# A scan on TensorE with split fp32r operands: two of its ten passes per output half joined in one pass on stacked rows

## The chip, the cores and the metric

The kernel runs on one core of a Trainium2 chip. TensorE (PE in the profile, with PEld for its weight loads) multiplies, VectorE (DVE), ScalarE (ACT) and GpSimd (POOL) do the elementwise work, and SyncE (SP) issues most DMAs. The engines run their own instruction streams and wait for each other through semaphores. The metric is the device time of one launch in microseconds. The kernel before took 4611.31 us, the median of three runs (4606.82 to 4611.5).

## The reference, cut to what matters

Two blocks follow each other. The first is the one that the change touches: it normalizes each 7 by 7 window of the image over its 192 channels, runs a linear recurrence over the 49 tokens of the window, and puts an MLP behind it.

```python
x = x + _L0_conv_ref(_gn(x), A, Bm, Cm, ...)     # block 1, group norm before it
x = x + _L1_conv_ref(_gn(x), qkv_w, ...)         # block 2, window attention

# inside block 1, w holds 1024 windows x 49 tokens x 192 channels:
w = _ln(w, ln1_w, ln1_b)
xs = jnp.swapaxes(w @ Bm, 0, 1)
h = xb + h @ A            # the scan, 49 steps, one after the other
w = h @ Cm
y = _ln(xr, ln2_w, ln2_b)
y = gelu(y @ W1 + b1) @ W2 + b2
return xr + y
```

## The kernel before

**Precision by parts.** An fp32 operand is held as an upper part rounded to fp32r and a lower part, what is left. A product is made from upper by upper, upper by lower and lower by upper. The contraction runs over 192 channels, which are 128 ("a") and 64 ("b"). `Split` keeps four weight tiles of 128 rows, `a_hi`, `a_lo`, `b_hi`, `b_lo`, and `Split.terms` lists five passes: (a_hi, da), (a_hi, dl), (a_lo, da), (b_hi, db), (b_lo, db). In the data tile slot 0 is the upper part of the first 128 channels; slot 1 holds the upper part of the last 64 channels in rows 0 to 63 and their lower part in rows 64 to 127. `b_hi` has the weights of those 64 channels twice, so that one pass takes both.

**Slots.** The scan has 49 steps, and each is cut in two chunks of 512 windows, so block 1 has 98 slots; the inner ones are a hardware loop (`Fori`), two slots a turn. Every engine has its own `slot(t, c)`, a list written out by hand with the pieces of several slots interleaved. Nothing but these lists and the semaphores sets the order. With n the slot's number, TensorE does in slot n:

1. the scan's sum for chunk step n+1 into `ps_h` (L618: two output halves of 128 and 64 channels, each 5 passes of `W_B` on xn and 5 of `W_A` on the state h, 20 in all, 512 columns each),
2. the transposes of `yb` into `ps_g` (L589, L591),
3. the second half of the MLP's second layer of n-1 into `ps_o` (L603),
4. the MLP's first layer, 30 passes into `ps_g` (L634), which wait for the lower parts of y (`s_yl`),
5. the state times `W_C` into `ps_r` (L645),
6. the transposes of `xn` of n+2 into `ps_h`,
7. the first half of the second layer (L603), which waits for all lower parts of the gelu's output (`s_gld`, `s_glp`).

The other engines, as far as the argument goes:

- ACT takes `ps_h` to `h_hi` with a bias (L401, `s_hh`), then `ps_g` to `y_hi` (L390, L391), then six gelus and their upper parts (L415, L420), then `ps_h` to `xn_hi` (L390, L391, `s_xh`).
- DVE normalizes the next tokens (L500 multiplies `xt` by a table, L502 subtracts another), makes the lower parts of h (L481) and of y (L479), finishes the output `x1` of the slot before (L488, L491, `s_x1`), then statistics and gelu lower parts (L531, L536, L543), then statistics of `ps_r` (L549, L554, L557), the lower parts of xn (L479), `res` (L564), `yb` (L568), and the other half of `x1` (L488, L491).
- POOL forms `res` (L442) and two reciprocal roots (L447, L456; the latter waits for L557), two gelu lower parts (L452), and behind L456 the square of `x1` and two running sums (L463, L465, L468).
- SP sends `x1` out in 14 DMAs as soon as `s_x1` says so (L379) and then loads the next `xt` (L351), in that order.

Of the kernel before, what the change touches and what calls it, by code (L numbers as in the profile page):

```python
# [7 lines left out]
fp32 = mybir.dt.float32  # L8
f32r = mybir.dt.float32r
# [47 lines left out]
def build(nc, x, A, Bm, Cm, ln1, ln2, W1, b1, W2, b2,  # L57
# [6 lines left out]
    with top:  # L64
# [31 lines left out]
        with ExitStack() as ctx:  # L96
# [6 lines left out]
            R1 = sb("R1", [P, NT, C])  # L103
            M1 = sb("M1", [P, NT, C])
            W_B, W_A, W_C = (Split(ctx, name, C) for name in ("wB", "wA", "wC"))
            W_1 = Split(ctx, "w1", HID)
            w2 = sb("w2", [P, FT, 2, C], f32r)
            b2b = sb("b2b", [P, C])
# [6 lines left out]
            with ExitStack() as pre:  # L115
# [49 lines left out]
                @block.gpsimd  # L165
                def _(pool):
                    pool.memset(acc_x[:, :, :], 0.0)
                    pool.memset(acc_x2[:, :, :], 0.0)
                    pool.memset(neg_half[:, :], -0.5).then_inc(s_i0, 1)
                    pool.wait_ge(s_i0, 1)  # L170

                    pool.wait_ge(s_wh, 1)
                    for full, parts in ((fold_B, W_B), (raw_A, W_A), (raw_C, W_C), (fold_1, W_1)):
                        for t in range(2):
                            pool.tensor_tensor(parts.parts[2 * t + 1][:, :], full[:, t, :],
                                               parts.parts[2 * t][:, :], ALU.subtract)
                    pool.tensor_tensor(w2[:, :, 1, :], raw_2[:, :, :], w2[:, :, 0, :], ALU.subtract)

                    pool.wait_ge(s_fold, 11)
                    pool.tensor_tensor(gtab[:, 0, :, :], gvar[:, :, :],  # L180
                                       neg_half[:, :].rearrange("p (a b) -> p a b", a=2), ALU.pow).then_inc(s_pow, 1)

                @block.vector
                def _(dve):
                    fold = [0]

                    def link(ins):

                        fold[0] += 1
                        ins.then_inc(s_fold, 1)  # L190
                        dve.wait_ge(s_fold, fold[0])

                    for k in range(NT):
                        if k == NT // 2:

                            dve.wait_ge(s_w, 16 * WEIGHT_LOADS)
                            for t in range(2):
                                dve.tensor_scalar(fold_B[:, t, :], raw_B[:, t, :], l1[:, t, 0:1], None, ALU.mult)
                                last = dve.tensor_scalar(fold_1[:, t, :], raw_1[:, t, :], l2[:, t, 0:1], None,
                                                         ALU.mult)  # L200
                            link(last)
                        dve.wait_ge(s_xs[k % XS], 16 * (k // XS + 1))
                        for g in range(GROUPS):
                            last = dve.bn_stats(st[:, GROUPS * k + g, :], xs[k % XS][:, :, CG * g:CG * (g + 1)])
                        last.then_inc(s_bn, 1)
                    dve.wait_ge(s_bn, NT)
                    per = T * CG / 2
                    link(dve.tensor_tensor(pm[:, 0, :], st[:, :, 1], st[:, :, 4], ALU.add))
                    link(dve.tensor_tensor(sq[:, 0, :], st[:, :, 1], st[:, :, 1], ALU.mult))
                    link(dve.tensor_tensor(sq[:, 1, :], st[:, :, 4], st[:, :, 4], ALU.mult))  # L210
                    link(dve.tensor_tensor(sq[:, 0, :], sq[:, 0, :], sq[:, 1, :], ALU.add))
                    link(dve.tensor_tensor(sq[:, 1, :], st[:, :, 2], st[:, :, 5], ALU.add))
                    link(dve.scalar_tensor_tensor(out=pm[:, 1, :], in0=sq[:, 1, :], scalar=1.0 / per,
                                                  in1=sq[:, 0, :], op0=ALU.mult, op1=ALU.add))

                    dve.wait_ge(s_sum, 1)
                    dve.tensor_copy(hbias[:, 0:1], ps_g[:, 0:1])
                    dve.tensor_copy(hbias[0:CB, 1:2], ps_g[0:CB, 1:2])
                    link(dve.tensor_tensor(b1f[:, :], ps_g[:, 8:8 + FT], b1c[:, :], ALU.add))
                    dve.wait_ge(s_sum, 2)  # L220
                    sums = ps_h[:, 0:8].rearrange("p (a h q) -> p a h q", a=2, h=2)
                    link(dve.tensor_scalar(gmean[:, :, :], sums[:, 0], 0.5, None, ALU.mult))
                    link(dve.tensor_tensor(gtab[:, 1, :, :], gmean[:, :, :], gmean[:, :, :], ALU.mult))
                    dve.scalar_tensor_tensor(out=gvar[:, :, :], in0=sums[:, 1], scalar=0.5,
                                             in1=gtab[:, 1, :, :], op0=ALU.mult, op1=ALU.subtract).then_inc(s_tab, 1)
                    dve.wait_ge(s_tab, 1)
                    link(dve.tensor_scalar(gvar[:, :, :], gvar[:, :, :], GN_EPS, None, ALU.add))
                    dve.wait_ge(s_pow, 1)
                    link(dve.tensor_tensor(gtab[:, 1, :, :], gmean[:, :, :], gtab[:, 0, :, :], ALU.mult))
                    link(dve.tensor_copy(gwide[:, :, :], gtab[:, :, :, :].rearrange("p a h q -> p (a h q)")  # L230
                                         .unsqueeze(2).to_broadcast([P, 8, WINS])))

                    dve.wait_ge(s_sum, 3)
                    for a, tab in enumerate((R1, M1)):
                        last = dve.tensor_copy(tab[:, :, :].rearrange("p k (g e) -> p (k g) e", e=CG),
                                               ps_g[:, 256 * a:256 * (a + 1)].unsqueeze(2)
                                               .to_broadcast([P, NT * GROUPS, CG]))
                    link(last)
# [40 lines left out]
            h_hi = [sb(f"h_hi{b}", [P, 2, NTOK], f32r) for b in range(2)]  # L279
            h_lo = [sb(f"h_lo{b}", [P, NTOK], f32r) for b in range(2)]  # L280
            yb = sb("yb", [P, TPC, C])
            y_hi, y_lo = sb("y_hi", [P, 2, NTOK], f32r), sb("y_lo", [P, NTOK], f32r)
            gF = [sb(f"gF{b}", [P, NTOK]) for b in range(4)]
            g_hi, g_lo = (sb(name, [P, FT, NTOK], f32r) for name in ("g_hi", "g_lo"))
# [27 lines left out]
            s_st1, s_ag1, s_ve1 = sem("ln1_stats"), sem("ln1_aggregated"), sem("ln1_var_eps")  # L312
            s_rs1, s_xn = sem("ln1_rstd"), sem("xn_ready")
            s_t1, s_xh, s_xl = sem("xn_transposed"), sem("xn_hi_ready"), sem("xn_lo_ready")
            s_scan, s_hh, s_hl = sem("scan_summed"), sem("h_hi_ready"), sem("h_lo_ready")
            s_cm, s_res, s_rsum = sem("mixed"), sem("residual_ready"), sem("residual_summed")
            s_st2, s_ag2, s_ve2 = sem("ln2_stats"), sem("ln2_aggregated"), sem("ln2_var_eps")
# [68 lines left out]
            def _(act):  # L386
# [6 lines left out]
                def slot(t, c):  # L393
# [13 lines left out]
                    if there(n):  # L407
                        for f in range(FT):
                            act.wait_ge(s_w1, FT * n + f + 1)
                            if f == 0:  # L410
                                upto(act, s_w2, n)
                            elif f >= 4:

                                act.wait_ge(s_gld, len(LO_DVE) * n + LO_DVE.index(f - 4) + 1)
                            act.activation(gF[f % 4][:, :], ps_g[:, f % 2, :], ACT.Gelu,  # L415
                                           bias=b1f[:, f:f + 1]).then_inc(s_gelu, 1)

                            for g in range(max(f - 1, 0), f + (f == FT - 1)):
                                act.wait_ge(s_gelu, FT * n + g + 1)
                                act.activation(g_hi[:, g, :], gF[g % 4][:, :], ACT.Copy).then_inc(s_gh, 1)  # L420
                    if there(n + 2):
                        act.wait_ge(s_t1, n + 3)
                        upto(act, s_scan, n + 1)
                        upper_parts(xn_hi[c], ps_h).then_inc(s_xh, 1)

                slots(act, slot)

            @block.gpsimd
            def _(pool):
                for c in range(2):  # L430
                    pool.memset(h_hi[c][:, :, :].bitcast(fp32), 0.0)
                    last = pool.memset(h_lo[c][:, :].bitcast(fp32), 0.0)
                last.then_inc(s_init, 1)

# [148 lines left out]
            def _(pe):  # L583
# [23 lines left out]
                def slot(t, c):  # L607
                    n = CHUNKS * t + c
                    if there(n + 1):

                        d = 1 - c
                        pe.wait_ge(s_xl, n + 2)
                        upto(pe, s_hl, n)
                        for m, rows in enumerate((P, CB)):
                            cols = slice(P * m, P * m + rows)
                            terms = (*W_B.terms(xn_hi[d], xn_lo[d], cols), *W_A.terms(h_hi[d], h_lo[d], cols))
                            for k, (w, v) in enumerate(terms):
                                last = pe.matmul(ps_h[0:rows, m, :], w, v, start=(k == 0), stop=(k == len(terms) - 1))  # L618
                        last.then_inc(s_scan, 1)
# [769 lines left out]
```

## Time and profile before

| what | us |
| --- | --- |
| median of three runs | 4611.31 |
| profiled execution, whole | 4597.89 |
| profiled execution, span from first to last instruction | 4596.1 |
| block 1, from the first xn (L500) to the last x1, about | 155 to 2430 |

The page of the profile gives busy time per engine over the span: PE 94%, weight loads 80%, DVE 86%, ACT 54%, POOL 56%. These are means over two very different blocks; only block 1 is touched by the change, so the rows of block 1 are the ones to read. A row of a timeline gives the start, the duration, the engine, the line and the shapes; what stands in brackets is how long the engine sat idle ahead of it and who ended that. A row of the windows gives the stretch and its length, then busy us and number of instructions of PE, PEld, DVE, ACT and POOL, then the granted TensorE clock as a share of full speed, the DMA share and GB/s. A busy matmul engine is shown by overlapping rows: a pass of 512 columns lasts 0.39 us in the trace, but the next one starts before it ends.

### The profile page before, as it was taken

The page shows a single profiled execution, that of the slowest core. Times are in us where ns is not written, and L with a number is a line of the kernel's source. Part 1 is how long each engine was busy: PE and PEld are TensorE (multiplying, and loading weights), DVE is VectorE, ACT ScalarE, POOL GpSimd, SP SyncE. Part 2 cuts the span into 40 slices and gives each one's busy share as a digit, 9 for nine tenths or more (in the row PEclk, how much of TensorE's full clock was granted, in tenths as well). Part 3 has the DMA queues.
Part 4 walks back from the last instruction along what each step waited for, and adds up shares of the span by engine and source line. Part 5 has one row for each costly group of instructions (what it writes and reads, how often), then busy time and mean ns, then how long its engine had stood idle before and what let it go on. Part 6 is the DMA issues. An engine that isn't in the chain of part 4 may idle for free. (4 is left out here: it accounts for less than half of the span.)

```text
span 4596.1 us, 142253 instructions
## 1 busy us (share of the span) xinstructions
PE 4316.2 (94%) x52232; PEld 3688.3 (80%) x52232; DVE 3933.2 (86%) x8105; ACT 2476.2 (54%) x4852; POOL 2584.1 (56%) x2092
## 2 busy tenths in 40 slices
PE   0599999999999999999995999999999999999998
PEld 0488888888888888888885888888888888888887
DVE  6698888888888888888872888888888888888888
ACT  0244444444444444444441666777776766776676
POOL 1155555555555555555542666666666666666666
PEclk9999999999999999999996999999999999999999
DMA  8011111111111111111111222222222222222222
GB/s 354 17 39 39 39 39 39 39 39 39 40 41 39 39 39 39 39 39 39 39 34 46 71 76 74 75 74 74 74 76 75 75 75 75 74 74 74 74 74 69
DMA packets 389849, 286.06 MB, mean 62 GB/s; under 512 B 147147, under 2 KB 388091, under 8 KB 388603
## 3 DMA queue, kind: packets, MB, share of 16 engines
q1 hardware_dynamic: 387060, 283.20, 21.2%
q10 hardware_dynamic: 2736, 2.14, 0.1%
q8 instruction: 35, 0.57, 0.1%
q14 instruction: 18, 0.15, 0.0%
HBM read 120.39 MB, written 87.31 MB: 45 GB/s over the span
## 5 line engine op out<-in xcount | busy, mean ns | idle before, releaser
L892 POOL TENSOR_TENSOR L<-L,mx 128x588 f32<-128x588 f32 x512 | 600.3, 1172 | 644.0 <-DVE mx L1118 643.9
L603 PE MATMUL ps_o<-w,g_hi 128*128 128x384 f32 x2352 | 711.1, 365 | 5.9 <-DVE g_lo L543 4.1
L415 ACT ACTIVATE gF<-ps_g,b1f 128x512 f32<-128x512 f32 x588 | 404.7, 688 | 392.9 <-PE ps_g L634 390.8
L886 POOL TENSOR_TENSOR E<-E,ri 128x588 f32<-128x588 f32 x512 | 600.0, 1172 | 0.8 <-DVE ri L1124 0.8
L1180 PE MATMUL ps_s<-Kp,Q 32*64 32x98 f32 x12288 | 494.5, 259 | 59.9 <-DMA Kp<-K 58.8
L603 PE MATMUL ps_o<-w,g_lo 128*128 128x192 f32 x2352 | 535.0, 255 | 0.0
L442 POOL TENSOR_TENSOR res<-xt,b2b 128x768 f32<-128x768 f32 x98 | 181.1, 1848 | 591.2 <-DVE x L491 591.2
L401 ACT ACTIVATE h_hi<-ps_h,hbias 128x512 fp32r<-128x512 f32 x196 | 123.1, 679 | 703.7 <-PE ps_h L618 703.7
L1114 DVE SCALAR_TENSOR_TENSOR L<-ps_s,bias 128x588 f32<-128x588 f32 x512 | 394.6, 771 | 92.2 <-PE ps_s L1180 76.5
L603 PEld LDWEIGHTS ps_o<-w,g_hi 128*128 128x128 f32 x2352 | 429.9, 189 | 26.8 <-issue 24.8
L999 ACT ACTIVATE o_hi<-ps_v,vb 128x98 fp32r<-128x98 f32 (+1 forms) x1024 | 289.1, 334 | 300.5 <-PE ps_v L1293 293.3
L603 PEld LDWEIGHTS ps_o<-w,g_lo 128*128 128x128 f32 x2352 | 444.2, 191 | 0.0
L974 ACT ACTIVATE PT<-ps_t 98x588 f32<-98x588 f32 x512 | 342.6, 669 | 157.5 <-PE ps_t L1256 154.5
L1180 PEld LDWEIGHTS ps_s<-Kp,Q 32*64 32x64 f32 x12288 | 299.7, 130 | 145.8 <-issue 37.1
L1118 DVE TENSOR_REDUCE mx<-L 128x12 f32<-128x588 f32 x512 | 392.2, 766 | 17.5
L1293 PEld LDWEIGHTS ps_v<-PT,Vx 98*32 98x32 f32 x12288 | 310.9, 151 | 95.8 <-issue 66.4
L1122 DVE TENSOR_REDUCE sm<-E 128x12 f32<-128x588 f32 x512 | 386.4, 755 | 0.1
L1293 PE MATMUL ps_v<-PT,Vx 98*32 98x49 f32 x12288 | 374.8, 235 | 4.0 <-DVE o_hi L1099 2.8
L452 POOL TENSOR_TENSOR g_lo<-gF,g_hi 128x512 fp32r<-128x512 f32 x196 | 250.4, 1298 | 197.2 <-ACT g_hi L420 197.2
L420 ACT ACTIVATE g_hi<-gF 128x512 fp32r<-128x512 f32 x588 | 355.4, 621 | 0.0
L980 ACT ACTIVATE E<-L 128x588 f32<-128x588 f32 x512 | 351.4, 686 | 3.9 <-POOL L L892 0.8
L536 DVE TENSOR_SCALAR xn<-xn,mva,rsa 128x192 f32<-128x192 f32 x392 | 316.6, 869 | 2.3 <-POOL rsa L447 2.3
(222 smaller groups left out, 12495.5 us busy)
## 6 DMA issues: line engine op xcount, KB each, us to landing
xs<-in_x SPq DMA_DIRECT2D x8, 4704.0 KB, 22.2
xt<-in_x SPq DMA_DIRECT2D x98, 384.0 KB, 3.4
x_cells<-x SPq DMA_DIRECT2D x784, 48.0 KB
xb<-x_cells SPq DMA_DIRECT2D x128, 294.0 KB
Vx<-V SPq DMA_DIRECT2D x512, 73.5 KB
out<-yo SPq DMA_DIRECT2D x128, 294.0 KB
Kp<-K SPq DMA_DIRECT2D x256, 98.0 KB, 2.0
Kp<-K SPq DMA_DIRECT2D x256, 49.0 KB, 1.9
```

The lines of the kernel that those rows point to most:

```text
L415: act.activation(gF[f % 4][:, :], ps_g[:, f % 2, :], ACT.Gelu, bias=b1f[:, f:f + 1]).then_inc(s_gelu, 1)
L420: act.activation(g_hi[:, g, :], gF[g % 4][:, :], ACT.Copy).then_inc(s_gh, 1)
L603: last = pe.matmul(dst, g[:, f, P * k:P * (k + 1)], w, start=(f == 0 and i == 0), stop=(f == FT - 1 and i == 1))
L886: pool.tensor_tensor(e, e, ri[p][:, :].unsqueeze(2).to_broadcast([P, HEADS, T]), ALU.mult)\
L892: pool.tensor_tensor(l, l, mx[p][:, :].unsqueeze(2).to_broadcast([P, HEADS, T]), ALU.subtract).then_inc(s_sub, 1)
L974: act.activation(PT[lp % 2][0:T2, :, :].rearrange("p j (w t) -> p w j t", w=2), ps_t[0:T2, :, 0:JP * SLOT].rearrange("p w (j t) -> p w j t ...
L980: act.activation(E[pp][:, :, :], L[pp][:, :, :], ACT.Exp).then_inc(s_ex, 1)
L1114: dve.scalar_tensor_tensor(out=L[p][:, :, :].rearrange("p (a h) m -> p a (h m)", a=2), in0=ps_s[:, :, 0:SB], scalar=HD ** -0.5, in1=tab, o ...
L1118: dve.tensor_reduce(mx[p][:, :], L[p][:, :, :], AX.X, ALU.max).then_inc(s_mx, 1)
L1122: dve.tensor_reduce(sm[pp][:, :], E[pp][:, :, :], AX.X, ALU.add).then_inc(s_sm, 1)
L1180: last = pe.matmul(s_pair(j)[SLOT * w:SLOT * (w + 1)], Q[c][rows, chunk, 2 * p + w, :], Kp[c][rows, chunk, :, 2 * p + w, :], start=True, s ...
L1293: last = pe.matmul(ps_v[row:row + 2 * HD, col:col + T], Vx[lc][0:T2, 2 * lp + w, g:2 * HD * JP:JP], PT[lp % 2][0:T2, j, T * w:T * (w + 1)] ...
```

## The change

The lower weight parts of the last 64 input channels (`W_B.b_lo`) and of the last 64 state channels (`W_A.b_lo`) each use only 64 rows of data. The change stacks them: a new weight tile `W_AB_b_lo` has `W_B`'s 64 rows on top and `W_A`'s below, and a new data tile `xh_b` (two buffers) has the upper part of xn's last 64 channels on top and that of h's below. One pass on the two tiles takes the place of two, for both output halves, so a slot has 18 scan passes for 20.

For this ACT makes two more copies per slot (64 partitions by 512 columns): the part of h behind the last gelu upper part, ahead of `xn_hi`; the part of xn behind `xn_hi`. TensorE's scan waits for two more semaphores. Before block 1, DVE makes `W_AB_b_lo` with two subtractions where POOL made two `b_lo` tiles, and POOL clears two more buffers at the start of block 1.

```diff
             W_B, W_A, W_C = (Split(ctx, name, C) for name in ("wB", "wA", "wC"))
+            W_AB_b_lo = sb("wAB_b_lo", [P, C], f32r)
...
-                        for t in range(2):
+                        for t in range(1 if parts in (W_A, W_B) else 2):
                             pool.tensor_tensor(parts.parts[2 * t + 1][:, :], full[:, t, :],
                                                parts.parts[2 * t][:, :], ALU.subtract)
...
+                    dve.wait_ge(s_wh, 1)
+                    for full, parts, rows in ((fold_B, W_B, slice(0, CB)), (raw_A, W_A, slice(CB, P))):
+                        dve.tensor_tensor(W_AB_b_lo[rows, :], full[rows, 1, :], parts.parts[2][rows, :], ALU.subtract)
                     dve.wait_ge(s_sum, 1)
...
+            xh_b = [sb(f"xh_b{b}", [P, NTOK], f32r) for b in range(2)]
...
+                    if there(n + 1):
+                        act.wait_ge(s_hh, n + 2)
+                        act.activation(xh_b[1 - c][CB:P, :], h_hi[1 - c][0:CB, 1, :], ACT.Copy).then_inc(s_hs, 1)
                     if there(n + 2):
                         act.wait_ge(s_t1, n + 3)
                         upto(act, s_scan, n + 1)
                         upper_parts(xn_hi[c], ps_h).then_inc(s_xh, 1)
+                        act.wait_ge(s_xh, n + 3)
+                        act.activation(xh_b[c][0:CB, :], xn_hi[c][0:CB, 1, :], ACT.Copy).then_inc(s_xs, 1)
...
                 for c in range(2):
                     pool.memset(h_hi[c][:, :, :].bitcast(fp32), 0.0)
+                    pool.memset(xh_b[c][:, :].bitcast(fp32), 0.0)
...
                         pe.wait_ge(s_xl, n + 2)
+                        pe.wait_ge(s_xs, n + 2)
                         upto(pe, s_hl, n)
+                        upto(pe, s_hs, n)
                         for m, rows in enumerate((P, CB)):
                             cols = slice(P * m, P * m + rows)
-                            terms = (*W_B.terms(xn_hi[d], xn_lo[d], cols), *W_A.terms(h_hi[d], h_lo[d], cols))
+                            terms = (*W_B.terms(xn_hi[d], xn_lo[d], cols)[0:4], *W_A.terms(h_hi[d], h_lo[d], cols)[0:4],
+                                     (W_AB_b_lo[:, cols], xh_b[d][:, :]))
```

On TensorE the first output half of one scan in the steady part stood like this before (a row is a pass, `out<-data,weights`; numbers behind a tile's name are its buffer):

```order
L618 MATMUL ps_h<-xn_hi0,wB_a_hi 128x512 [waits h_lo_ready,xn_lo_ready]
L618 MATMUL ps_h<-xn_lo0,wB_a_hi 128x512
L618 MATMUL ps_h<-xn_hi0,wB_a_lo 128x512
L618 MATMUL ps_h<-xn_hi0,wB_b_hi 128x512
L618 MATMUL ps_h<-xn_hi0,wB_b_lo 128x512
L618 MATMUL ps_h<-h_hi0,wA_a_hi 128x512
L618 MATMUL ps_h<-h_lo0,wA_a_hi 128x512
L618 MATMUL ps_h<-h_hi0,wA_a_lo 128x512
L618 MATMUL ps_h<-h_hi0,wA_b_hi 128x512
L618 MATMUL ps_h<-h_hi0,wA_b_lo 128x512
```

The same place in the changed kernel, where the line is L633:

```order
L633 MATMUL ps_h<-xn_hi0,wB_a_hi 128x512 [waits h_lo_ready,h_b_hi_stacked,xn_b_hi_stacked,xn_lo_ready]
L633 MATMUL ps_h<-xn_lo0,wB_a_hi 128x512
L633 MATMUL ps_h<-xn_hi0,wB_a_lo 128x512
L633 MATMUL ps_h<-xn_hi0,wB_b_hi 128x512
L633 MATMUL ps_h<-h_hi0,wA_a_hi 128x512
L633 MATMUL ps_h<-h_lo0,wA_a_hi 128x512
L633 MATMUL ps_h<-h_hi0,wA_a_lo 128x512
L633 MATMUL ps_h<-h_hi0,wA_b_hi 128x512
L633 MATMUL ps_h<-xh_b0,wAB_b_lo 128x512
```

Ten passes have become nine; the second output half (64x512) changes in the same way. The first pass waits for two semaphores more, and nothing else on TensorE has moved.

On ACT the end of one slot stood like this before, from the last gelu upper part to the state's upper part of the next slot:

```order
L420 ACTIVATE g_hi<-gF1 128x512 [waits hidden_ready]
L390 ACTIVATE xn_hi0<-ps_h 128x512 [waits scan_summed,xn_transposed]
L391 ACTIVATE xn_hi0<-ps_h 64x512
L401 ACTIVATE h_hi0<-ps_h,hbias 128x512 [waits mixed,scan_summed]
L401 ACTIVATE h_hi0<-ps_h,hbias 64x512
L390 ACTIVATE y_hi<-ps_g 128x512 [waits y_transposed]
```

In the changed kernel:

```order
L426 ACTIVATE g_hi<-gF1 128x512 [waits hidden_ready]
L429 ACTIVATE xh_b1<-h_hi1 64x512 [waits h_hi_ready]
L396 ACTIVATE xn_hi0<-ps_h 128x512 [waits scan_summed,xn_transposed]
L397 ACTIVATE xn_hi0<-ps_h 64x512
L435 ACTIVATE xh_b0<-xn_hi0 64x512 [waits xn_hi_ready]
L407 ACTIVATE h_hi0<-ps_h,hbias 128x512 [waits mixed,scan_summed]
L407 ACTIVATE h_hi0<-ps_h,hbias 64x512
L396 ACTIVATE y_hi<-ps_g 128x512 [waits y_transposed]
```

One copy now stands ahead of `xn_hi`, in the place where ACT waits for TensorE's transposes, and one between `xn_hi` and the next state.

## Rows read from the trace of the kernel before

**Rows 1.** Busy time by engine (windows) in a stretch of block 1's steady part.

```profile
1000.00:1500.00 500.00, 499.97 (x2942) 430.90 (x2941) 443.77 (x940) 226.82 (x396) 251.65 (x177) 1.00 0.14 39
```

**Rows 2.** Timeline of PE and PEld, one scan and its neighbours, then the next first layer.

```profile
1215.86 0.39 PE L618 MATMUL ps_h<-xn_hi,wB_a_hi 128*128 128x512 f32 x1
...
1220.45 0.60 PE L589 MATMUL ps_g<-ident,yb 128*128 128x128 f32 x4
...
1224.92 0.19 PEld L634 LDWEIGHTS ps_g<-y_hi,w_a_hi 128*128 128x128 f32 x1 [0.24 <-DVE y_hi L479]
```

**Rows 3.** Timeline of ACT in the same slot.

```profile
1210.00 1.14 ACT L420 ACTIVATE g_hi<-gF 128x512 fp32r<-128x512 f32 x2
1212.42 0.60 ACT L390 ACTIVATE xn_hi<-ps_h 128x512 fp32r<-128x512 f32 x1 [1.28 <-PE ps_h L591]
1212.92 0.58 ACT L391 ACTIVATE xn_hi<-ps_h 64x512 fp32r<-64x512 f32 x1
1220.65 1.26 ACT L401 ACTIVATE h_hi<-ps_h,hbias 128x512 fp32r<-128x512 f32 x2 [7.15 <-PE ps_h L618]
```

**Rows 4.** Timeline of DVE in the same slot.

```profile
1210.92 1.28 DVE L543 TENSOR_TENSOR g_lo<-gF,g_hi 128x512 fp32r<-128x512 f32 x2
...
1213.87 0.68 DVE L479 TENSOR_TENSOR xn_lo<-ps_h,xn_hi 128x512 fp32r<-128x512 f32 x1
...
1219.57 1.38 DVE L500 TENSOR_TENSOR xn<-xt,R 128x768 f32<-128x768 f32 x1 [0.73 <-DMA xt<-in_x]
1220.98 0.96 DVE L502 TENSOR_TENSOR xn<-xn,M 128x768 f32<-128x768 f32 x1
1221.94 0.75 DVE L481 SCALAR_TENSOR_TENSOR h_lo<-ps_h,hbias,h_hi 128x512 fp32r<-128x512 f32 x1
...
1224.18 0.68 DVE L479 TENSOR_TENSOR y_hi<-ps_g,y_hi 64x512 fp32r<-64x512 f32 x1
...
1242.46 1.27 DVE L500 TENSOR_TENSOR xn<-xt,R 128x768 f32<-128x768 f32 x1 [0.83 <-DMA xt<-in_x]
```

**Rows 5.** Timeline of POOL, the last sum of this slot and of the next.

```profile
1218.27 1.87 POOL L468 TENSOR_TENSOR acc_x<-acc_x,x1sq 128x768 f32<-128x768 f32 x1
...
1241.06 1.86 POOL L468 TENSOR_TENSOR acc_x<-acc_x,x1sq 128x768 f32<-128x768 f32 x1
```

**Rows 6.** Timeline of DVE and ACT, the slot in which xt came latest.

```profile
308.21 0.96 DVE L500 TENSOR_TENSOR xn<-xt,R 128x768 f32<-128x768 f32 x1 [1.40 <-DMA xt<-in_x]
...
308.62 1.26 ACT L401 ACTIVATE h_hi<-ps_h,hbias 128x512 fp32r<-128x512 f32 x2 [7.15 <-PE ps_h L618]
...
309.20 0.96 DVE L502 TENSOR_TENSOR xn<-xn,M 128x768 f32<-128x768 f32 x1
...
310.08 0.74 DVE L481 SCALAR_TENSOR_TENSOR h_lo<-ps_h,hbias,h_hi 128x512 fp32r<-128x512 f32 x1
```

**Rows 7.** One tile (xn) from 1000 to 1500 us: duration ns min/median/max.

```profile
L500 DVE TENSOR_TENSOR xn<-xt,R x22: 1048/1270/1432, 1014.5 to 1493.1; 128x768 f32<-128x768 f32 x22
```

**Rows 8.** Groups by line, 1000 to 1500 us (busy, mean ns, idle before in all).

```profile
L481 DVE SCALAR_TENSOR_TENSOR h_lo<-ps_h,hbias,h_hi 128x512 fp32r<-128x512 f32 x22 | 16.5, 751 | 0.2
```

**Rows 9.** Timeline of DVE, the ramp's third scan, then block 1's last.

```profile
218.92 0.75 DVE L481 SCALAR_TENSOR_TENSOR h_lo<-ps_h,hbias,h_hi 128x512 fp32r<-128x512 f32 x1 [1.18 <-ACT h_hi L401]
...
2384.37 0.75 DVE L481 SCALAR_TENSOR_TENSOR h_lo<-ps_h,hbias,h_hi 128x512 fp32r<-128x512 f32 x1 [3.10 <-ACT h_hi L401]
```

**Rows 10.** Timeline of PE in the ramp's first scan.

```profile
167.18 0.80 PE L618 MATMUL ps_h<-xn_hi,wB_a_hi 128*128 128x512 f32 x1 [2.65 <-DVE xn_hi L479]
...
170.34 0.63 PE L618 MATMUL ps_h<-h_hi,wA_a_lo 128*128 128x512 f32 x1
170.76 0.60 PE L618 MATMUL ps_h<-h_hi,wA_b_hi 128*128 128x512 f32 x1
```

**Rows 11.** Timeline of DVE ahead of block 1.

```profile
142.76 0.16 DVE L222 TENSOR_SCALAR gmean<-ps_h 128x4 f32<-128x4 f32 x1 [1.71 <-PE ps_h L258]
```

**Rows 12.** Busy time by engine (windows) at block 1's end.

```profile
2395.00:2405.00 10.00, 8.56 (x63) 7.93 (x62) 7.48 (x20) 2.38 (x5) 7.02 (x5) 1.00 0.08 22
```

More of the change, by code:

```diff
@@ L314, in build @@
             s_t1, s_xh, s_xl = sem("xn_transposed"), sem("xn_hi_ready"), sem("xn_lo_ready")
+            s_xs, s_hs = sem("xn_b_hi_stacked"), sem("h_b_hi_stacked")
             s_scan, s_hh, s_hl = sem("scan_summed"), sem("h_hi_ready"), sem("h_lo_ready")
```

## The prediction

> **What bounds the kernel now.** I read the stretch windows first. From 1000 to 1500 us, a steady piece of block 1, TensorE is busy for 499.97 of 500 us, DVE for 443.77, ACT for 226.82 and POOL for 251.65 [rows 1]. Read alone, that says that TensorE is the bound and that every pass taken from it is time gained. Matmul records overlap, however, so this number cannot show small waits. So I went to the timelines and followed one slot, looking at each wait for what ends last.
>
> TensorE does wait. The first weight load of the MLP's first layer sits idle for 0.24 us until DVE's lower part of y is there (L479 ends at 1224.18 + 0.68 = 1224.86) [rows 2, 4]. DVE reaches that point by a fixed run of four pieces that starts with the lower part of h (L481) at 1221.94 [rows 4]. What lets L481 start? Two paths lead from the end of DVE's last gelu lower part (L543: 1210.92 + 1.28 = 1212.20) [rows 4] to this one instruction:
>
> - *Path T, by TensorE.* Half a second layer, then the scan from 1215.86, whose successor starts at 1220.45 [rows 2]; ACT makes the upper part of h from 1220.65 to 1221.91 [rows 3]; L481 starts 0.03 us behind it [rows 4].
> - *Path P, by POOL.* DVE's statistics, then POOL's root, square and two sums, the last of which ends at 1218.27 + 1.87 = 1220.14 [rows 5]. DVE's L500 ends at 1219.57 + 1.38 = 1220.95, then L502 at 1220.98 + 0.96 = 1221.94, and L481 starts at 1221.94 [rows 4].
>
> L500 is marked as having waited for its load, but its end is not set by that. It ends 0.81 us behind POOL's last sum here; one slot later, starting 0.10 us later against the slot, it ends at 1242.46 + 1.27 = 1243.73, again 0.81 us behind POOL's 1241.06 + 1.86 = 1242.92 [rows 4, 5]. Where the load comes so late that POOL is through, L500 takes 0.96 us [rows 6]; in the steady part it takes 1.05 to 1.43 [rows 7]. The excess of 0.09 to 0.47 us is time in which it cannot proceed beside POOL, and that much slack has the load. The Trainium skill, page "SBUF — State Buffer", section "Who interferes with whom", calls the port pair that the two engines share an exclusive lock; by that rule L500 would stand until POOL's sum is done, and the trace agrees.
>
> Behind L481 both paths are one again: y's lower parts, TensorE's first layer, gelus, POOL's gelu lower parts, L543. One turn takes 22.79 us (POOL's last sum starts at 1218.27 and at 1241.06) [rows 5]. Only path T contains the scan. So what the change is worth hangs on how much shorter path P is.
>
> **How much shorter path P is.** L481 starts 0.00 us behind the end of L502, on average 0.2 / 22 = 0.01 [rows 4, 8]. Where DVE has nothing to wait for, it starts earlier than that: in the slot with the late load ACT was through at 308.62 + 1.26 = 309.88, and L481 started at 310.08 while L502 ended at 309.20 + 0.96 = 310.16, that is 0.08 us ahead of the end [rows 6]. So in the steady slots L481 waits for ACT for about 0.08 us, and path P is shorter by that. It is a small difference read from one place, so its bounds are 0 (L481 is released by L502 already) and 0.10. I take 0.08.
>
> **The change part by part.**
>
> *Passes.* A pass costs (1220.45 - 1215.86) / 20 = 0.2295 us [rows 2]; four fewer take 0.92 us out of path T in each slot. Of this 0.08 us moves L481 forward; then path P ends last, and the other 0.84 us becomes a longer wait of TensorE ahead of the first layer: 0.24 + 0.84 = 1.08 us. There are 98 scans; three belong to the ramp and one is the last, so the steady term is 94 x 0.08 = 7.5 us, with bounds 0 and 9.4.
>
> *Ramp.* In the first three scans DVE waits for the state, in the third, where it waits least, for 1.18 us, which is more than 0.92 [rows 9]; no POOL sum is under way then. The passes there run at two rates. In the first scan the early ones come every 0.42 us (170.34 to 170.76), behind a wait of 2.65 us [rows 10]: the lower of the clock's two levels, against 0.2295. I take the rise of the clock as not moved by the change, so that fast passes fall away: 3 x 0.92 = 2.8 us. If slow ones fell away in two scans, it would be 2 x 1.7 + 0.92 = 4.3.
>
> *Last scan.* No further L500 stands in its way, and DVE waits 3.10 us for it [rows 9]: 0.9 us.
>
> *Copies on ACT.* The trace has no copy from SBUF to SBUF of this shape. The nearest rows are 0.58 us for 64 partitions from PSUM and 1.14 for two of 128 from SBUF [rows 3]. The first copy stands ahead of `xn_hi`, where ACT is idle for 1.28 us until TensorE's transposes end [rows 3]; it ends 0.7 us before them. Even when late it would cost nothing at first, as DVE takes up `xn_hi` at 1213.87, 0.37 us behind its end at 1213.50 [rows 3, 4]. Without any cover, 0.6 us would go into path T, which after the cut has 0.84 to give. The second copy ends near 1213.50 + 0.65 = 1214.15, and TensorE wants it at 1215.86 [rows 2, 3]; behind it ACT idles for 7.15 us in the row of before [rows 3]. Both cost 0. If a copy took 1.7 us instead, it would begin to hold DVE up; no row of ACT with 512 columns is near that.
>
> *Two more waits on TensorE's scan.* Both semaphores have risen 1.7 us earlier by the sum above. Bounds 0 and the few hundredths that a released instruction starts late, and these fall into the 1.08 us. Queued behind the scan's first pass are all of TensorE's passes; they have the same cover. Cost 0.
>
> *Ahead of block 1.* Two subtractions of 64x192 on DVE stand before a wait of 1.71 us for TensorE [rows 11]. Their nearest row is the one of 64x512, 0.68 us [rows 4]; two of that would be 1.36, so the wait hides them. POOL has less to do there and clears two more buffers while DVE waits for its first load. Cost 0.
>
> **Sum.** 7.5 + 2.8 + 0.9 = 11.2 us, with bounds 0 + 2.8 + 0.9 = 3.7 and 9.4 + 4.3 + 0.9 = 14.6. Against the profiled execution, 4597.89 us, that is 4586.7, or 0.24% less. The median of the runs shown is 4611.31, 0.3% above that execution; the same 11.2 us from it give 4600.
>
> **A rule weighed against the row.** By the matmul row, 499.97 of 500, TensorE is the bound and the sum would be 90 us (first rival). The Trainium skill, page "Perfetto Trace Analysis", section "Identifying the Most-Contended Engine", says that matmul occupancy is a bad measure and that the share of weight loads is a good one for TensorE, while occupancy is fair for the others. Here that is 430.90 / 500 = 86% against DVE's 443.77 / 500 = 89% [rows 1]: by that rule DVE is the most contended and a cut on TensorE alone gives about nothing. The chain read above lands nearer to the rule than to the row.
>
> **The rivals.**
>
> *TensorE is the bound after all.* Then each slot gains the whole 0.92 us: 94 x 0.92 + 3.7 = 90 us, 4521. For it: its wait of 0.24 us is 1% of a slot [rows 2]. Against it: L500 ends at the same distance behind POOL in both slots shown, and L502 ends where L481 starts; the POOL path would have to give way by itself. 6 in 100.
>
> *The two paths are equally long.* L481 is released by L502 as well, and only the ramp and the last scan gain: 3.7 us, 4607.6. For it: 0.00 us between L502 and L481. Against it: the 0.08 us of overlap in the late slot. A load that comes too late in the shorter slots leads to the same place; its slack is 0.09 us at the least. 18 in 100.
>
> *Slower: TensorE's clock falls in the new wait.* The wait ahead of the first layer grows to 1.08 us. Behind a wait of 2.65 us at least eight passes ran at the lower level [rows 10]; eight times 0.42 - 0.23 is 1.5 us, on the path itself, in each slot: 94 x 1.5 less 11 is some 130 us, 4741. It decides as soon as a wait of about 1 us is enough for the clock to fall. Against it: at block 1's end TensorE was busy for 8.56 of 10 us, idle for 1.44, and the granted clock stayed 1.00 [rows 12]; here it would idle for 1.1 in 22.7. 4 in 100.
>
> **How the numbers follow.** The forecast (path P takes over, 3.7 to 14.6 us gained, 11.2 taken) has 72 in 100. Its time is 4600, and its own range with the spread of the runs (about 2 us to a side) is 4595 to 4609. The range 4592 to 4610 takes in the second case too; beyond it lie the first and third rival, 10 in 100, and a tenth of the rest. About 0.2% (9.2 us) is what a measurement of this kernel can tell from no change. The forecast lies just above that: I give 0.7 of it to faster and the rest to the same. Faster: 0.72 x 0.7 + 0.06, with a little of the second case, 0.57. Slower: the third rival and a little for what is not seen, 0.05. Same: 0.38.
>
> **What would show it.** In the changed profile a slot of block 1 takes about 22.71 us for 22.79. L481 starts 0.08 us ahead of L502's end, with ACT's state done almost 0.9 us earlier. TensorE's first layer waits about 1.08 us for y, and the scan takes 18 x 0.2295 = 4.13 us. L500 still ends 0.81 us behind POOL's last sum. If slots take 21.9 us, I misread what ends L500; if they take 22.79, the 0.08 us was none; if the granted clock drops below 1.00 in the steady part, it is the third rival.

## The result, and the profile after

The changed kernel took 4594.93 us (median of 7 runs, 4587.64 to 4599.72) against 4606.82 us for the kernel before in the same runs. The ratio is 0.9971 with a 95% interval of 0.9959 to 0.9982: 0.29% faster, about 13 us (8 to 19 by the interval). Forecast were 11.2 us. The forecast time of 4600 was taken from a median of 4611.31 us; in the runs compared here the kernel before stood at 4606.82, and that accounts for 4.5 of the 5 us between 4600 and 4594.93.

In the windows of the same stretch TensorE is no longer busy without a break; columns as in [rows 1]:

```profile
1000.00:1500.00 500.00, 491.88 (x2909) 425.24 (x2908) 445.99 (x947) 256.14 (x442) 253.55 (x177) 1.00 0.14 39
```

TensorE has lost 8 us of 500, the granted clock is still 1.00. The view of the tile xn in the same stretch gives the slot, from the first and the last of its 22 starts:

```profile
L512 DVE TENSOR_TENSOR xn<-xt,R x22: 1087/1344/1528, 1009.9 to 1486.7; 128x768 f32<-128x768 f32 x22
```

(1486.7 - 1009.9) / 21 = 22.70 us. Before it was (1493.1 - 1014.5) / 21 = 22.79 [rows 7]. The rest is in the timeline of one slot, here with the rows of all engines in order of time. L512, L514 and L493 on DVE are L500, L502 and L481 of before, L480 is POOL's last sum (L468), L633 the scan, and L429 and L435 are the two copies:

```profile
1205.71 0.63 ACT L429 ACTIVATE xh_b<-h_hi 64x512 fp32r<-64x512 f32 x1
...
1206.97 0.60 ACT L396 ACTIVATE xn_hi<-ps_h 128x512 fp32r<-128x512 f32 x1 [0.63 <-PE ps_h L603]
...
1208.07 0.63 ACT L435 ACTIVATE xh_b<-xn_hi 64x512 fp32r<-64x512 f32 x1
...
1210.41 0.39 PE L633 MATMUL ps_h<-xn_hi,wB_a_hi 128*128 128x512 f32 x1
...
1212.82 1.84 POOL L480 TENSOR_TENSOR acc_x<-acc_x,x1sq 128x768 f32<-128x768 f32 x1
...
1213.98 1.50 DVE L512 TENSOR_TENSOR xn<-xt,R 128x768 f32<-128x768 f32 x1 [0.58 <-DMA xt<-in_x]
...
1214.55 0.60 PE L601 MATMUL ps_g<-ident,yb 128*128 128x128 f32 x4
...
1214.75 1.26 ACT L407 ACTIVATE h_hi<-ps_h,hbias 128x512 fp32r<-128x512 f32 x2 [6.04 <-PE ps_h L633]
...
1215.51 0.96 DVE L514 TENSOR_TENSOR xn<-xn,M 128x768 f32<-128x768 f32 x1
...
1216.39 0.75 DVE L493 SCALAR_TENSOR_TENSOR h_lo<-ps_h,hbias,h_hi 128x512 fp32r<-128x512 f32 x1
...
1218.63 0.68 DVE L491 TENSOR_TENSOR y_hi<-ps_g,y_hi 64x512 fp32r<-64x512 f32 x1
...
1219.36 0.19 PEld L649 LDWEIGHTS ps_g<-y_hi,w_a_hi 128*128 128x128 f32 x1 [0.59 <-DVE y_hi L491]
...
1235.54 1.86 POOL L480 TENSOR_TENSOR acc_x<-acc_x,x1sq 128x768 f32<-128x768 f32 x1
...
1236.94 1.27 DVE L512 TENSOR_TENSOR xn<-xt,R 128x768 f32<-128x768 f32 x1 [0.83 <-DMA xt<-in_x]
```

Against [rows 2 to 5] the reader is to see four things. L493 now starts 0.08 us ahead of L514's end (1215.51 + 0.96 = 1216.47), where L481 started 0.00 behind it. ACT's state is there at 1214.75 + 1.26 = 1216.01, 0.38 us ahead of L493, where it was 0.03 ahead. L512 ends 0.82 us behind POOL's sum in this slot (1213.98 + 1.50 against 1212.82 + 1.84) and 0.81 behind it in the next, although it starts at different distances. This is no matter of one slot: in all 22 slots between 1000 and 1500 us L512 ends 0.81 or 0.82 us behind the sum, as L500 did, and L493 starts 0.08 or 0.09 us ahead of L514's end, where L481 started 0.00 or 0.01 us behind L502's. And the scan takes 1214.55 - 1210.41 = 4.14 us, 0.45 less than before, of which 0.35 went to a longer wait ahead of the first layer, 0.59 for 0.24 (over the 22 slots 0.62 on average, for 0.25).

The profiled execution as a whole does not show the gain: its span is 4597.5 us against 4596.1. Block 1, from the first xn to the last x1, did get shorter: from 155.26 to 2419.11 after, 2263.85 us, against 154.78 to 2430.35, 2275.57 us, before. The rest, block 2 with the same instructions, took 4597.5 - 2419.11 = 2178.4 us against 2165.8. In windows of it the granted clock of the changed kernel's execution is lower near the end:

```profile
4200.00:4400.00 200.00, 193.39 (x3628) 163.50 (x3626) 171.18 (x335) 135.61 (x288) 133.27 (x121) 0.97 0.26 72
4400.00:4597.00 197.00, 184.52 (x3556) 156.00 (x3550) 166.90 (x332) 130.76 (x279) 129.79 (x117) 0.96 0.26 71
```

Before, the same two windows had 0.99 each. That this belongs to the execution and not to the change is shown by the experiments below: two executions with the changed scan of 18 passes had block 2 in 4587.2 - 2420.85 = 2166.3 us (early_load_after) and in 4576.8 - 2392.40 = 2184.4 us (late_sum_after). So in what follows I read the slot's length from the profile and the whole from the ratios.

### The profile page after: what moved, and what is told of

It reads as the page before. It is cut to its first block and busy times, and to the rows that moved or that the text cites. A ratio compares the mean times of both kernels' runs of the same rounds, so it can differ in the third digit from the quotient of the medians.

```text
span 4597.5 us, 142157 instructions
## 1 busy us (share of the span) xinstructions
PE 4282.9 (93%) x52036; PEld 3664.4 (80%) x52036; DVE 3935.5 (86%) x8107; ACT 2601.8 (57%) x5048; POOL 2584.3 (56%) x2092
```

## The experiments

Ratios are to the kernel before in the same runs, with their 95% interval. "Slot" is (last start - first start) / (count - 1) of the first xn instruction between 1000 and 1500 us, as above.

| kernel | scan passes | ratio | slot, us | block 1 ends at |
| --- | --- | --- | --- | --- |
| before | 20 | 1 | 22.79 | 2430.35 |
| changed | 18 | 0.9971 (0.9959 to 0.9982) | 22.70 | 2419.11 |
| copies_only | 20 | 0.9994 (0.9983 to 1.0005) | 22.78 | 2429.13 |
| scan16 | 14 | 0.9964 (0.9950 to 0.9979) | 22.69 | 2414.30 |
| short_sum_before | 20 | 1.0011 (1.0001 to 1.0020) | 22.80 | 2431.26 |
| short_sum_after | 18 | 0.9925 (0.9908 to 0.9941) | 22.39 | 2389.55 |
| late_sum_after | 18 | 0.9911 (0.9894 to 0.9927) | 22.40 | 2392.40 |
| late_sum_before | 20 | 0.9999 (0.9988 to 1.0010) | 22.78 | 2427.83 |
| early_load_after | 18 | 0.9965 (0.9951 to 0.9979) | 22.71 | 2420.85 |
| early_late_after | 18 | 0.9882 (0.9865 to 0.9898) | 22.35 | 2384.20 |
| early_late_before | 20 | 0.9988 (0.9979 to 0.9998) | 22.78 | 2426.87 |
| early_late_16 | 14 | 0.9716 (0.9700 to 0.9732) | 21.54 | 2306.47 |

The theory: the slot ends with the later of two paths to DVE's h_lo, one through the scan, one through POOL's sums and L500; with 20 passes the first is 0.08 us longer, with 18 the second rules. On the second path POOL can hold L500 only while L500 executes: directly ahead of it the program has DVE wait for the load and for TensorE's transposes (`s_x`, `s_t1`), not for POOL. The chief rival: the two copies or the two waits took back what the passes gave.

**copies_only.** The changed kernel with its twenty passes back; for them POOL makes the two `b_lo` tiles again ahead of block 1.

```diff
-                        for t in range(1 if parts in (W_A, W_B) else 2):
+                        for t in range(2):
...
-                            terms = (*W_B.terms(xn_hi[d], xn_lo[d], cols)[0:4], *W_A.terms(h_hi[d], h_lo[d], cols)[0:4],
-                                     (W_AB_b_lo[:, cols], xh_b[d][:, :]))
+                            terms = (*W_B.terms(xn_hi[d], xn_lo[d], cols), *W_A.terms(h_hi[d], h_lo[d], cols))
```

> The changed kernel with its twenty passes back: ACT still makes both copies, TensorE still waits for both new semaphores, and DVE still makes the stacked weight tile, but the stacked tiles are not multiplied. My theory (the copies and waits lie under cover; the scan's path through TensorE is the one that ends last with 20 passes): slot 22.79 us as before, ratio 1.000, within 0.1%. Rival (each slot gave back 0.4 us of its gain to the copies or the waits, which is why 2 passes of 0.23 us saved only 0.07 us a slot): slot about 23.1 to 23.2 us, some 35 us slower, ratio 1.008.

The slot is 22.78 us, 0.01 less than before, and the ratio holds 1. The copies take 0.63 us each and lie where ACT had been idle. The rival falls: copies and waits cost nothing with 20 passes, and early_late_after below has them too and keeps nearly the whole gain of its passes.

**scan16.** Passes left out of the changed scan.

```diff
-                            terms = (*W_B.terms(xn_hi[d], xn_lo[d], cols)[0:4], *W_A.terms(h_hi[d], h_lo[d], cols)[0:4],
+                            terms = (*W_B.terms(xn_hi[d], xn_lo[d], cols)[0:4:3], W_B.terms(xn_hi[d], xn_lo[d], cols)[1],
+                                     *W_A.terms(h_hi[d], h_lo[d], cols)[0:4:3], W_A.terms(h_hi[d], h_lo[d], cols)[1],
```

> The changed kernel with 16 passes per scan: the two products of the lower weight parts of the first 128 channels are left out for both operands and both halves, which is part of the computation. My theory (the path over POOL's sums and DVE's L512 ends last once the scan is shorter): slot 22.72 us as in the changed kernel, TensorE's wait for y grows from 0.59 to about 1.5 us, and only the ramp and the last scan gain, some 3 us; ratio to before about 0.996 to 0.997. Rival (TensorE's amount of work is what counts): 4 passes of 0.23 us fewer take 0.92 us from each slot, 21.8 us, ratio 0.978. Second rival (the granted clock falls in a wait of 1.5 us): slots longer than 22.8 us and a granted clock below 1.00 in the steady part.

The name and the expectation miscount: what is left out is one pass per operand and output half, four in all, so 14 remain of 18. The slot is 22.69 us, 0.01 less than with 18 passes, for 0.92 us less work. The waits between 1000 and 1500 us (total, times, longest) show where it went:

```profile
PEld ps_g L650 <- DVE y_hi L491: 33.4, 22, 1.5
```

TensorE now waits 33.4 / 22 = 1.52 us a slot ahead of the first layer, and the granted clock of that stretch stayed 1.00:

```profile
1000.00:1500.00 500.00, 472.23 (x2823) 411.38 (x2822) 446.36 (x952) 256.61 (x441) 253.21 (x177) 1.00 0.14 39
```

The column of the granted clock alone would not be enough. In the kernel before it says 1.00 for the start of the first scan, where the passes come every 0.42 us [rows 10], and 0.50 for a piece of the second scan, where they come every 0.43:

```profile
167.00:171.00 4.00, 3.82 (x9) 3.04 (x10) 2.04 (x3) 0.00 (x0) 0.00 (x0) 1.00 0.00 0
186.00:190.00 4.00, 4.00 (x11) 2.93 (x11) 3.86 (x7) 0.00 (x0) 0.00 (x0) 0.50 0.37 98
```

So the rate has to agree with it. Behind the long wait of scan16 it does: the passes come every 0.23 us from the second on, the rate of the steady part. That answers the rival of the falling clock, at a wait two and a half times as long as the change made it. The timeline of PE in scan16, first layer:

```profile
1215.52 0.50 PE L650 MATMUL ps_g<-y_hi,w_a_hi 128*128 128x512 f32 x1 [1.25 <-DVE y_hi L491]
1215.85 0.40 PE L650 MATMUL ps_g<-y_lo,w_a_hi 128*128 128x512 f32 x1
1216.09 0.40 PE L650 MATMUL ps_g<-y_hi,w_a_lo 128*128 128x512 f32 x1
1216.32 0.39 PE L650 MATMUL ps_g<-y_hi,w_b_hi 128*128 128x512 f32 x1
```

**short_sum_before and short_sum_after.** POOL's sum of x1 on 4 of 192 columns, in both kernels, which leaves out most of that sum.

```diff
-                        a = acc_x[:, TPC * d:TPC * (d + 1), :]
-                        pool.tensor_tensor(a, a, x1[d][:, :, :], ALU.add).then_inc(s_acc1, 1)
+                        a = acc_x[:, TPC * d:TPC * (d + 1), 0:4]
+                        pool.tensor_tensor(a, a, x1[d][:, :, 0:4], ALU.add).then_inc(s_acc1, 1)
```

> The kernel before with POOL's running sum of x1 (L465) made on 4 of 192 columns, which leaves out most of that sum; POOL's chain to the next L500 is 1.7 us shorter. My theory (with 20 passes the scan's path ends last, by some 0.08 us): slot stays at 22.79 us, ratio 1.000; L500 takes about 0.96 us and L481 starts with a real wait for ACT. Rival (the paths were equal and the POOL path rules in both kernels, or L500 is ruled by its load): slot shorter by some 0.1 us or more, or L500 unchanged in its end.

> The changed kernel with the same sum on 4 of 192 columns. My theory: with POOL's chain out of the way the two saved passes count in full, and the slot goes to the scan's path with 18 passes, 22.79 - 0.46 = 22.33 us, or to the load of xt where that comes late, at most 22.5; ratio to before 0.981 to 0.989. Rival (L512's end has another cause than POOL's sums): slot stays 22.72 us.

With 20 passes nothing is gained (22.80 us), and DVE's h_lo now waits for ACT, which it did not visibly before; L500 takes 0.96 us throughout. The tile view and the waits of short_sum_before:

```profile
L500 DVE TENSOR_TENSOR xn<-xt,R x22: 957/959/961, 1015.1 to 1493.8; 128x768 f32<-128x768 f32 x22
```

```profile
DVE h_lo L481 <- ACT h_hi L401: 7.7, 20, 0.7
```

With 18 passes the same edit brings 22.70 - 22.39 = 0.31 us a slot. This settles both halves of the theory: POOL's sums set the end of L500, and they rule only where the scan is short. The expected slot came, the expected ratio did not: 0.9925 lies outside 0.981 to 0.989. A slot shorter by 0.40 us is 98 x 0.40 = 39 us of 4603, a ratio of 0.9915, so the expectation's ratios had not been worked out from its slots.

**late_sum_after and late_sum_before.** The whole computation; POOL's last sum goes to the start of its next slot, behind L514.

```diff
+                def squares(n, c):
+                    pool.wait_ge(s_sq, n)
+                    a = acc_x2[:, TPC * c:TPC * (c + 1), :]
+                    pool.tensor_tensor(a, a, x1sq[:, :, :], ALU.add).then_inc(s_acc2, 1)
...
+                    if there(n - 2):
+                        if there(n + 2):
+                            pool.wait_ge(s_gn, n + 3)
+                        squares(n - 1, c)
...
-                        pool.wait_ge(s_sq, n)
-                        a = acc_x2[:, TPC * d:TPC * (d + 1), :]
-                        pool.tensor_tensor(a, a, x1sq[:, :, :], ALU.add).then_inc(s_acc2, 1)
```

> The changed kernel with the whole computation; only POOL's last sum (L480) moves to the start of POOL's next slot, behind DVE's L514, where POOL was idle for 6 us. Theory: L512 and L514 no longer stand behind a POOL sum, L512 ends when its load has landed plus 0.96 us (0.1 to 0.5 us earlier than now), and the slot is the later of the scan's path (22.33 us) and the load's: 22.35 to 22.6 us, ratio to before 0.982 to 0.992. Rival (L512's end is not POOL's doing): 22.72 us. Second rival (the moved sum blocks another DVE instruction): 22.8 us or more.

> The kernel before with the same move and 20 passes. Theory: the scan's path ends last, so the slot stays 22.79 us, ratio 1.000. If the move alone brought what late_sum_after shows, the passes would not matter: then this one would be as fast as that one.

Both as the theory has it: 22.40 us with 18 passes, 22.78 us (no change) with 20. The ratio of 0.9911 is within what was expected. The tile views of late_sum_after and late_sum_before:

```profile
L519 DVE TENSOR_TENSOR xn<-xt,R x23: 957/959/961, 1000.3 to 1493.2; 128x768 f32<-128x768 f32 x23
```

```profile
L507 DVE TENSOR_TENSOR xn<-xt,R x22: 957/958/961, 1014.2 to 1492.5; 128x768 f32<-128x768 f32 x22
```

The first instruction takes 0.96 us in every slot of both, so nothing holds it once it has begun; only with the shorter scan does the slot become shorter, (1493.2 - 1000.3) / 22 = 22.40 us.

**early_load_after.** The load ahead of the stores, in the changed kernel (SP's stores belong to the next slot number, with one more slot at the end).

```diff
-                    if there(n - 1):
-                        d, u = (1 - c), (t if c else t - 1)
+                    if there(n - 2):
+                        d, u = c, t - 1
...
-                        sp.wait_ge(s_x1, n)
+                        sp.wait_ge(s_x1, n - 1)
```

> The changed kernel, whole computation; SP issues the load of xt ahead of the 14 stores of x1 and not behind them, so that xt is there some 10 us before L512. Theory: L512 starts 0.08 us ahead of L503's end and overlaps POOL's last two sums; if POOL's sum keeps it from proceeding its end stays 0.81 us behind that sum and the slot stays 22.72 us. Rival (the load ruled L512): slot shorter by some 0.3 us. If L512 gets in between POOL's two sums, POOL's last sum is late instead and the slot may shrink by a few tenths.

The slot stays at 22.71 us although L513 has no wait for a load any more. It starts at 1214.75 and lasts 2.18 us, to 0.81 us behind POOL's sum (1214.26 + 1.86 = 1216.12). The timeline of this kernel, and its tile view:

```profile
1214.26 1.86 POOL L481 TENSOR_TENSOR acc_x<-acc_x,x1sq 128x768 f32<-128x768 f32 x1
...
1214.75 2.18 DVE L513 TENSOR_TENSOR xn<-xt,R 128x768 f32<-128x768 f32 x1
```

```profile
L513 DVE TENSOR_TENSOR xn<-xt,R x22: 2066/2130/2202, 1010.4 to 1487.3; 128x768 f32<-128x768 f32 x22
```

So the load set when L500 and L512 started, as the bracket in their rows says, but not when they ended. The Trainium skill, page "SBUF — State Buffer", section "Who interferes with whom", has the shared port pair as an exclusive lock; 0.96 us of work stretched to 2.13 behind a sum that had started 0.49 us earlier agrees. That the end comes 0.81 us behind the sum's recorded end and not the full 0.96 is not explained by any run here; and no run tells the port from another cause by which POOL's sum could hold this instruction.

**early_late_after, early_late_before and early_late_16.** Both moves, by the edits shown for late_sum_after and early_load_after, with 18, 20 and 14 passes.

> The changed kernel, whole computation, with both moves: POOL's last sum behind L514 and the load ahead of the stores. Theory: L512 depends on neither, so only the scan's path is left: slot 22.33 us, ratio to before 0.981. Rival: another wait takes over (the load's buffer free later, stores later) and the slot stays above 22.5 us.

> The kernel before (20 passes) with both moves of early_late_after: POOL's last sum behind L502 and the load of xt ahead of the stores; whole computation. Theory (the scan's path alone is left in both, so now the passes count in full): slot 22.79 us, ratio 1.000, against 22.35 us for early_late_after, that is 2 x 0.23 us apart. Rival (the two moves bring the gain and the passes little): slot near 22.4 us.

> early_late_after with 16 passes per scan; the products of the lower weight parts of the first 128 channels are left out. Theory: the scan's path is still the one that ends last, with 0.73 us of DVE waiting for ACT to give, so the slot falls by another 0.46 us to 21.9 us, ratio to before about 0.972; DVE's wait in front of h_lo falls from 0.73 to about 0.27 us. Rival (another path takes over right below 22.35 us): slot stays at 22.3 us.

With 18 passes the slot is 22.35 us and the ratio 0.9882, the fastest kernel here that makes the whole computation. With 20 it is 22.78 us, so that two passes are worth 0.43 us, nearly their full 0.46. The ratio expected for 18 passes, 0.981, was missed in the same way as above: 0.44 us a slot are 98 x 0.44 = 43 us, 0.9906. The measured 0.9882 (0.9865 to 0.9898) is even a little more than that, and more than the 46 us by which block 1 ends earlier in the profile; where the rest comes from is open. The tile view of early_late_after, then the groups by line of early_late_after and of early_late_before between 1000 and 1500 us (busy, mean ns, idle before):

```profile
L520 DVE TENSOR_TENSOR xn<-xt,R x22: 948/954/959, 1018.3 to 1487.7; 128x768 f32<-128x768 f32 x22
```

```profile
L501 DVE SCALAR_TENSOR_TENSOR h_lo<-ps_h,hbias,h_hi 128x512 fp32r<-128x512 f32 x22 | 16.5, 751 | 16.0 <-ACT h_hi L408 16.0
L489 DVE SCALAR_TENSOR_TENSOR h_lo<-ps_h,hbias,h_hi 128x512 fp32r<-128x512 f32 x22 | 16.5, 750 | 26.2 <-ACT h_hi L402 26.2
```

h_lo now waits 16.0 / 22 = 0.73 us for the scan's path; with 20 passes it waits 26.2 / 22 = 1.19 us, 0.46 more. early_late_16 has 14 passes too, the same miscount, and the ratio in its expectation does not follow from the slot beside it (21.9 us would be some 0.98). Four passes fewer are 0.92 us, of which DVE had 0.73 to give plus the 0.08 of a start without a wait: 0.81, and the slot fell by 22.35 - 21.54 = 0.81 us. The other 0.1 us went into TensorE's wait ahead of the first layer (6.1 / 23 = 0.27 us in early_late_after, 8.4 / 23 = 0.37 here). There h_lo has no idle time ahead of it any more (same view as L501 above):

```profile
L501 DVE SCALAR_TENSOR_TENSOR h_lo<-ps_h,hbias,h_hi 128x512 fp32r<-128x512 f32 x23 | 17.1, 744 | 0.0
```

## Why the prediction was right, and which terms were not

*What bounds the kernel.* Right, and shown from both sides: shortening POOL's chain alone gives 0 (short_sum_before, late_sum_before), shortening the scan alone gives 0.09 us a slot by two passes (changed) and 0.10 by six (scan16), and with POOL's chain shortened or moved the same two passes are worth 0.41 (short_sum), 0.38 (late_sum) or 0.43 us (early_late).

*The steady term, 94 x 0.08 = 7.5 us.* Right. From the ramp's third h_lo to the last one of block 1 the time went from 2165.45 (218.92 to 2384.37) to 2157.53 us (217.02 to 2374.55), 7.9 less, and this has the last scan's 0.46 in it; 7.5 remain. How close the agreement is should not be overrated: the same stretch took 2164.26 to 2166.84 us in the five kernels with 20 passes, and 2157.04 us in early_load_after, whose slot is that of the changed kernel. The 0.08 us that I had read from one late slot is what DVE now shows in the row of L493.

*The pass count.* Wrong, and the one step that failed. I took four passes out of the slot. Ten passes per half have become nine, so it is two, 0.46 us and not 0.92; TensorE's instructions fell by 196 = 2 x 98. The rows that I had printed said so. The steady term did not suffer, because it is the smaller of the cut and 0.08 us, but everything that hangs on the full cut did: the wait ahead of the first layer is 0.59 us in the slot shown and 0.62 on average, not 1.08 (0.24 + 0.46 - 0.08 = 0.62 with the right count), the scan takes 18 passes as I wrote but ACT's state is 0.38 us early, not almost 0.9, and the first rival would have been 94 x 0.46, some 45 us, not 90.

*Ramp, 2.8 us, and last scan, 0.9 us.* Both mis-sized by the same miscount: the right sums are 1.4 and 0.46, so that the whole should have read 7.5 + 1.4 + 0.5 = 9.4 us. Measured were 2.4 for the ramp (from the first xn to the third h_lo 64.14 and 61.76 us), 0.5 for the last scan and 1.4 behind it; with the steady 7.5 that is 11.7 us for block 1. The surplus in the ramp goes with the clock, in these two executions. In the first scan 9 of 20 passes came at the lower rate before [rows 10] and 11 of 18 after, so that the first scan gained nothing; in the second it was 14 before and 10 after, and it gained 1.29 us. That belongs to the executions and not to the change: of its 20 passes there early_late_before has only 10 at the lower rate, and copies_only 14 again. The timeline of PE in the changed kernel's first scan, where the rate changes behind its twelfth pass:

```profile
167.65 0.79 PE L633 MATMUL ps_h<-xn_hi,wB_a_hi 128*128 128x512 f32 x1 [2.65 <-DVE xn_hi L491]
...
172.08 0.63 PE L633 MATMUL ps_h<-xn_lo,wB_a_hi 128*64 128x512 f32 x1
172.51 0.50 PE L633 MATMUL ps_h<-xn_hi,wB_a_lo 128*64 128x512 f32 x1
172.85 0.39 PE L633 MATMUL ps_h<-xn_hi,wB_b_hi 128*64 128x512 f32 x1
173.08 0.39 PE L633 MATMUL ps_h<-h_hi,wA_a_hi 128*64 128x512 f32 x1
```

From first xn to third h_lo the five kernels with 20 passes took 64.14, 64.71, 63.91, 63.40 and 63.09 us, those with 18 passes 61.76, 62.36, 62.52, 62.80 and 61.43: the ramp scatters by 1.4 to 1.6 us without any change of the scan, and the means are 1.7 us apart. From the last h_lo to the last x1 it was 45.98, 44.52, 45.33, 44.42 and 44.53 against 44.56, 44.54, 45.47, 45.21 and 44.54, so the 1.4 us behind the last scan are scatter of the same kind. The profiled execution of the kernel before had the longest end of all ten, 45.98 us. Against copies_only, with 20 passes and all else of the changed kernel, block 1 is shorter by 2273.61 - 2263.85 = 9.8 us, close to the 9.4. So it is luck that the forecast of 11.2 stands beside 11.7: a count that was double met scatter in the same direction. The measured ratio is too coarse (0.9959 to 0.9982, 8 to 19 us) to tell 9.4 from 11.2.

*Copies, waits and the part ahead of block 1 at no cost.* Right (copies_only). The copy lasts 0.63 us, and 0.63 us of ACT's 1.28 us gap are left. The margin behind that was smaller than written: path T had 0.38 us to give, not 0.84, and an uncovered copy of 0.63 us would have cost an estimated 0.25 us a slot (0.63 - 0.38).

*The clock as the slower rival.* It did not come; at two and a half times the wait (1.52 us, scan16) the granted clock in the steady part was still 1.00 and the passes came every 0.23 us. The row that it was priced from was a poor likeness: the passes at the lower rate in the first scan had not only a wait of 2.65 us ahead of them but, before a few transposes, one of 15.11 us.

*The rule against the row.* The matmul row said TensorE, the rule of the Trainium skill (page "Perfetto Trace Analysis", section "Identifying the Most-Contended Engine") said DVE, and a cut of six passes on TensorE moved the slot by 0.10 us: the rule came nearer. Its remedy, to work on the most contended engine, is not what helped, however. early_late_after leaves DVE's instructions as they are and gains 1.2%, by the cut of two passes on TensorE together with the move of one POOL instruction and one load. The moves without the cut leave the slot at 22.78 us (early_late_before), the cut without the moves at 22.70.

## What to carry to other kernels

An engine that is busy for 100% in the trace may still have another path of equal length beside it. Before costing a cut, find the one instruction where the paths meet and see which of its predecessors ends last, and by how much; in the steady part the cut is worth no more than that difference. The bracket of a row says what released the instruction's start and nothing of its end: here a DVE instruction whose start moved and whose end stayed 0.81 us behind a POOL instruction was held by POOL. And count the removed instructions in the order of both kernels, not from the words of the change.

## What the runs showed that I had not expected

- The two ways of taking POOL out of the path differ little: the shortened sum gives 22.39 us a slot and the moved one 22.40. With xt loaded early as well it is 22.35: once POOL is out of the way, the load takes a last 0.05 us.
- Block 2, whose instructions are the same in all kernels, took between 2165 us (late_sum_before) and 2184 us (late_sum_after) in the executions profiled, a spread larger than the whole effect of the change. The whole time of one profiled execution of each kernel could not have decided this case.
- Freed of POOL and of its load, L520 takes 0.95 us, and TensorE is again at 499.76 of 500 us in the windows of early_late_after, nearly the 499.97 of the kernel before [rows 1], at a slot 0.44 us shorter.
